# Token stage of a conv and Fourier-mixing block: norm sums of half chunks in single partitions, one row operation on 224 columns

## The chip, the cores and the metric

One NeuronCore of one Trainium2 chip runs the whole kernel. The time is the device time of one launch in microseconds (us). A core has the engines PE (matrix multiplication, with its weight loads shown as PEld), DVE (vector), ACT (scalar activations), POOL (GpSimd) and SP, which here issues every DMA. Each engine works through its own instructions in order; semaphores tie them together.

## The reference

Input `x` is 32 images of 96 channels by 56 x 56 pixels. Layer 0 is a convolution block (1x1, depthwise 3x3 and 1x1 convolutions with batch norms) added to `x`. Layer 1 works on tokens: each image has 3136 tokens of 96 channels.

```
t = _to_tokens(x)                              # (32, 3136, 96)
t = t + attn(_ln_t(t), ...)                    # w1, relu, FFT over tokens, diagonal + relu, inverse FFT, w2
t = t + ffn(_ln_t(t), W1, b1, W2, b2)          # 96 -> 384 -> 96 with fp8-like rounding

def _ln_t(v, eps=1e-5):
    m = jnp.mean(v, axis=-1, keepdims=True)
    s = jnp.var(v, axis=-1, keepdims=True)
    return (v - m) / jnp.sqrt(s + eps)
```

The change is in how the mean and the variance of the two `_ln_t` are made: for each of an image's 3136 tokens a mean and a standard deviation over 96 channels.

## The kernel before

The convolution stages run first, over all images, and leave the input of the last batch norm in HBM. The change is in `tokens_stage`, which then does layer 1 image by image. Channels lie in partitions there and tokens in columns; an image is 7 chunks of CH = 448 columns (`NCH` = 7).

**The pipeline.** An image passes through these steps: load and batch norm (`load_in`, `bn3`, `pool_y`), first norm (`square1`, `mean1`, `var1`, `std1`, `row1`), first product and first half of the FFT (14 groups: `w1`, `rstd1`, `h`, `stage1`, `a`), a round trip of `a` through HBM (`store_a`, `load_b`), spectrum (6 groups: `spectrum`, `scaled`, `real`, `imag`, `relu`, `fold`), product with w2 and first inverse half (8 groups: `w2`, `wz`, `stage3`, `c`), a round trip of `c` through HBM (`store_c`, `load_d`, 4 pieces), `stage4` and `residual` (7 chunks), second norm (`square2`, `mean2`, `var2`, `std2`, `rstd2`, `spread_mean`, `centre`, `spread_rstd`, `norm`) and the two MLP products (`mlp1` 21 times, `mlp2` 7 times, with their copies and biases).

**The order.** The table `PLACES` gives each step a place on a line of 5 x 2000 places. In a turn (there are 36) every engine goes through places 0 to 1999 and at place s does the steps that stand at s, s + 2000, ... s + 8000, the last of these for images that are 1 to 4 behind. So five images are in work at once, and the table fixes the order of instructions on each engine. A place is no time: each engine does its next instruction as soon as its semaphores allow it. Sorted by place, the orders around the first norm are in each turn:

```
PE   ... spectrum 0, mlp2 5, spread_rstd 3, w2 7, mlp1 18, 19, stage3 7, mlp1 20, spectrum 1,
     mean1 0, square1 0, mlp2 6, mean1 1, square1 1, w1 0, spectrum 2, stage4 0, w1 1, stage1 0, ...
ACT  ... mlp2 copy 5, h16 18, 19, relu 0, h16 20, scaled 1, mean1 0, square1 1, mlp2 copy 6, std1 0, relu 1, mean1 1, scaled 2, ...
DVE  ... c 7, bias1 19, fold 0, bias1 20, relu1 6, var1 0, real 1, ...
SP   ... store_c 3, load_t 5, load_in 1, row1 0, load_t 6, load_d 3, store_out, load_b 3, load_in 2, row1 1, ...
```

`h16` is the copy of an `mlp1` result by ACT; `relu1` and `bias1` are the DVE's part of the MLP. `w1 0` waits for the rows that `row1` sends, `stage4 0` for all four `load_d` of its image. `load_d 3` waits on SP for the landing of `store_c 3`, which waits for `c 7` (the DVE's copy of `stage3 7`).

**The sums (lines 1284 to 1316).** PE multiplies a chunk (or its square, made by ACT) with `mean_w[:, 0:32]`, 96 x 32 values of 1/96. Chunk 4r + q goes to output partitions 32q to 32q + 31, all of which get the same row of 448 sums. So round r = 0 takes chunks 0 to 3 and round r = 1 chunks 4 to 6. Means go to PSUM bank `L0`, sums of squares to `L1`. [...]

**The row operations.** For each round ACT squares the means (`m2a`, `m2b`; for the second norm it also copies them to `mrow`), DVE subtracts (line 1661) and clips at zero (line 1663), and ACT takes the root (line 1497 or 1502), all on 128 x 448 or 96 x 448. For the first norm SP then sends one row per chunk to partition 96 of `y` (line 1208), where it meets `w1a`; for the second norm DVE takes the reciprocal (line 1730) and PE spreads mean and reciprocal over 96 partitions by a matmul with one row of ones (`row1`, line 1321), two chunks at a time from two different row groups.

**Waits that matter.** `mean1` round 1 waits for `var1` round 0, since both use `L0`. `square1` round 1 on ACT waits for PE's sums of round 0, since both use the buffer `sq`.

Of the kernel before, what the change touches and what calls it, by code (L numbers as in the profile page):

```python
# [98 lines left out]
def build(nc, x4, cw1, g1, b1, cw2, g2, b2, cw3, g3, b3, aw1, bn1g, bn1b, bn1m, bn1v, ar, ai, arb, aib,
          aw2, bn2g, bn2b, bn2m, bn2v, fw1, fb1, fw2, fb2, t1_d, t4_d, g2_d, g3_d, ident_d, lane_d, out4):  # L100
# [929 lines left out]
PLACES = {'load_in': (0, 143, 286, 429, 571, 714, 863),  # L1030
 'act_bn3': (341, 496, 576, 750, 888, 1052, 1183),
 'pool_y': (362, 517, 597, 771, 909, 1074, 1204),
 'store_t': (1247,),
 'act_square1': (1683, 2129),
 'mean1': (2073, 2154),
 'square1': (2092, 2169),
 'act_mean1': (2117, 2210),
 'dve_var1': (2135, 2289),
 'act_std1': (2171, 2329),
 'row1': (2189, 2347),  # L1040
 'w1': (2289, 2391, 2443, 2495, 2569, 2775, 2860, 2933, 3060, 3116, 3234, 3309, 3398, 3460),
 'dve_rstd1': (2314, 2414, 2466, 2518, 2641, 2820, 2904, 3025, 3084, 3152, 3272, 3331, 3424, 3487),
 'act_h': (2356, 2422, 2474, 2533, 2650, 2830, 2915, 3040, 3098, 3161, 3290, 3367, 3438, 3521),
 'stage1': (2407, 2459, 2585, 2695, 2877, 2949, 3005, 3132, 3266, 3343, 3414, 3476, 3552, 3630),
 'act_a': (2435, 2487, 2634, 2719, 2904, 2973, 3029, 3174, 3313, 3380, 3450, 3533, 3576, 3654),
 'store_a': (2502, 2734, 2988, 3189, 3395, 3548, 3669),
 'load_b': (3765, 3781, 3901, 4264),
 'spectrum': (3897, 4032, 4326, 4731, 5023, 5149),
 'act_scaled': (3948, 4079, 4377, 4797, 5068, 5221),
 'dve_real': (3995, 4159, 4417, 4835, 5110, 5433),  # L1050
 'pool_imag': (3986, 4118, 4415, 4835, 5103, 5250),
 'act_relu': (4030, 4188, 4512, 4866, 5134, 5495),
 'dve_fold': (4058, 4242, 4649, 5041, 5247, 5516),
 'w2': (4511, 4821, 4966, 5189, 5507, 5690, 5795, 5969),
 'dve_wz': (4557, 4867, 5029, 5235, 5571, 5736, 5841, 5990),
 'stage3': (4678, 4894, 5097, 5289, 5594, 5754, 5864, 6007),
 'dve_c': (4722, 4918, 5156, 5334, 5672, 5778, 5928, 6039),
 'store_c': (4934, 5351, 5795, 6048),
 'load_d': (5035, 5481, 6020, 6241),
 'load_t': (5469, 5531, 5706, 5743, 5963, 6068, 6230),  # L1060
 'stage4': (6371, 6424, 6476, 6551, 6602, 6659, 6712),
 'dve_residual': (6397, 6449, 6501, 6576, 6627, 6684, 6737),
 'act_square2': (6595, 6766),
 'mean2': (6621, 6791),
 'square2': (6641, 6807),
 'act_mean2': (6666, 6843),
 'dve_var2': (6698, 6879),
 'act_std2': (6728, 6928),
 'dve_rstd2': (6752, 6958),
 'spread_mean': (6911, 7324, 7611, 7881),  # L1070
 'spread_rstd': (7077, 7379, 7671, 7959),
 'dve_centre': (6930, 6944, 7345, 7359, 7638, 7652, 7908),
 'dve_norm': (7094, 7137, 7396, 7410, 7688, 7708, 7976),
 'mlp1': (7177, 7183, 7228, 7250, 7260, 7283, 7431, 7437, 7493, 7501, 7546, 7569, 7729, 7735, 7771, 7777, 7834, 7840,
          7995, 8001, 8026),
 'act_h16': (7198, 7210, 7244, 7263, 7275, 7303, 7461, 7484, 7510, 7543, 7559, 7586, 7742, 7754, 7783, 7794, 7847,
             7857, 8008, 8020, 8052),
 'dve_bias1': (7216, 7227, 7276, 7284, 7292, 7322, 7478, 7501, 7536, 7583, 7592, 7603, 7760, 7770, 7800, 7811, 7863,
               7873, 8030, 8042, 8086),
 'dve_relu1': (7300, 7373, 7549, 7616, 7820, 7887, 8100),  # L1080
 'mlp2': (7361, 7443, 7576, 7647, 7847, 7941, 8127),
 'act_o': (7389, 7473, 7601, 7671, 7871, 7981, 8159),
 'dve_bias2': (7427, 7490, 7666, 7702, 7922, 8025, 8188),
 'pool_out': (7438, 7502, 7677, 7714, 7934, 8038, 8199),
 'store_out': (8253,)}
# [724 lines left out]
```

## Time and profile before

| | us |
|---|---|
| median of 3 runs (5497.74 to 5525.28) | 5508.2 |
| the profiled execution | 5526.98 |
| its span | 5525.2 |
| PE busy | 5073.0 (92%) |
| DVE busy | 3675.9 (67%) |
| ACT busy | 3496.6 (63%) |
| POOL busy | 2539.9 (46%) |

PE busy time is modelled from pipelined matmuls, so a busy PE need not be one at its peak. The token stage starts at about 2572.85 us (its first DMA) and lasts to the end.

### The profile page before, as it was taken

The page shows a single profiled execution, that of the slowest core. Times are in us where ns is not written, and L with a number is a line of the kernel's source. Part 1 is how long each engine was busy: PE and PEld are TensorE (multiplying, and loading weights), DVE is VectorE, ACT ScalarE, POOL GpSimd, SP SyncE. Part 2 cuts the span into 40 slices and gives each one's busy share as a digit, 9 for nine tenths or more (in the row PEclk, how much of TensorE's full clock was granted, in tenths as well). Part 3 has the DMA queues.
Part 4 walks back from the last instruction along what each step waited for, and adds up shares of the span by engine and source line. Part 5 has one row for each costly group of instructions (what it writes and reads, how often), then busy time and mean ns, then how long its engine had stood idle before and what let it go on. Part 6 is the DMA issues. An engine that isn't in the chain of part 4 may idle for free.

```text
span 5525.2 us, 146982 instructions
## 1 busy us (share of the span) xinstructions
PE 5073.0 (92%) x59604; PEld 3360.4 (61%) x59604; DVE 3675.9 (67%) x6406; ACT 3496.6 (63%) x5895; POOL 2539.9 (46%) x1508
## 2 busy tenths in 40 slices
PE   8999999999999899996798989999999999999986
PEld 8955555555555444443566666666667666666663
DVE  1167776776778667774277777777777676777765
ACT  4456555665665588884466766666667666666652
POOL 0077777777777556663233333333333333333321
PEclk9999999999999999998699999999999999999986
DMA  7667776776776799996456566565565655656441
GB/s 161 154 156 190 180 188 177 191 190 173 187 188 178 233 418 417 419 417 233 139 145 172 153 169 171 159 177 154 167 174 155 169 151 162 171 159 177 144 119 47
DMA packets 500652, 1061.12 MB, mean 192 GB/s; under 512 B 178048, under 2 KB 346976, under 8 KB 466976
## 3 DMA queue, kind: packets, MB, share of 16 engines
q1 hardware_dynamic: 499984, 1051.72, 64.1%
q8 instruction: 479, 7.85, 0.6%
q14 instruction: 189, 1.55, 0.1%
HBM read 552.39 MB, written 478.94 MB: 187 GB/s over the span
## 4 chain that ended last, share of the span: by engine, by line
PE 35%; ACT 5%; DMA 4%; issue 4%; DVE 3%; SPq 1%; POOL 1%; DVEq 0%; POOLq 0%; ACTq 0%
PE bank_w L1412 5%; PE bank_s L1421 5%; PE bank_x L1367 4%; PE bank_o L1392 4%; PE bank_l L1321 4%; DMA bt<-a_scratch 3%; PE bank_c L1375 2%; PE bank_c L1376 2%; PE bank_x L1364 2%; PE bank_o L1403 2%; PE bank_l L1348 2%; ACT h L1487 1%; PE bank_c L1382 1%; DMA y<-va 1%; PE bank_l L1309 1%
## 5 line engine op out<-in xcount | busy, mean ns | idle before, releaser
L762 POOL TENSOR_TENSOR hlo<-h,hhi 128x1682 f16<-128x1682 f32 x288 | 977.4, 3394 | 381.7 <-DVE hhi L815 381.7
L775 DVE BATCH_NORM_STATS2 stats<-z 128x6 f32<-128x392 f32 x1152 | 597.1, 560 | 443.2 <-ACT z L715 433.1
L725 ACT ACTIVATE h<-c1ps,s 128x1568 f32<-128x1568 f32 x288 | 479.1, 1663 | 631.5 <-PE c1ps L641 631.5
L673 PE MATMUL dwps<-hhi,taps 64*64 64x392 f16 x13824 | 692.2, 331 | 11.4 <-issue 11.4
L673 PE MATMUL dwps<-hlo,taps 64*64 64x392 f16 x13824 | 684.2, 328 | 7.4 <-issue 7.4
L1606 POOL TENSOR_TENSOR y<-zin,x_tok 96x448 f32<-96x448 f32 x224 | 254.1, 1135 | 791.1 <-ACT zin L1562 790.8
L1622 POOL TENSOR_TENSOR onat<-tb,o 96x448 f32<-96x448 f32 x224 | 237.7, 1061 | 784.8 <-DVE o L1682 784.8
L920 ACT ACTIVATE z2m<-z2m,s 128x784 f32<-128x784 f32 x512 | 489.3, 1029 | 103.1 <-DMA z2m<-z_scratch 102.8
L1412 PE MATMUL bank_w<-w1a,y 97*112 97x193 f32 x1792 | 410.7, 354 | 137.1 <-DMA y<-va 102.8
L673 PEld LDWEIGHTS dwps<-hhi,taps 64*64 64x64 f16 x13824 | 382.5, 106 | 251.0 <-issue 106.0
L944 POOL TENSOR_TENSOR h_split<-z2m,h_split 128x1568 f16<-128x1568 f32 x128 | 405.1, 3165 | 263.8 <-DVE h_split L983 263.8
L673 PEld LDWEIGHTS dwps<-hlo,taps 64*64 64x64 f16 x13824 | 407.5, 106 | 186.6 <-issue 10.5
L1556 ACT ACTIVATE h<-bank_w,rt 112x192 f32<-112x192 f32 x896 | 326.2, 418 | 206.5 <-PE bank_s L1421 129.9
L1412 PEld LDWEIGHTS bank_w<-w1a,y 97*112 97x112 f32 x1792 | 287.6, 185 | 264.2 <-DMA y<-va 129.9
L1613 POOL TENSOR_TENSOR s_plus<-d_minus,imag_scaled 128x448 f32<-128x448 f32 (+1 forms) x192 | 231.9, 1208 | 470.2 <-ACT imag_scaled L1472 470.2
L1487 ACT ACTIVATE h<-bank_l 128x448 f16<-128x448 f32 x672 | 342.5, 546 | 148.7 <-PE bank_l L1348 145.6
L1421 PE MATMUL bank_s<-h,t1c 112*128 112x192 f32 x1792 | 385.9, 338 | 3.4 <-ACT a L1549 3.4
L1669 DVE TENSOR_SCALAR h<-h,fqb 128x448 f16<-128x448 f16 x672 | 302.1, 468 | 121.4 <-ACT h L1487 108.2
L956 PE MATMUL pps<-z2m,w3T 128*96 128x392 f32 x1024 | 362.5, 497 | 15.1 <-ACT z2m L920 15.1
L193 POOL TENSOR_TENSOR xlo<-xin,x_packed 96x448 f16<-96x448 f32 x224 | 233.9, 1045 | 287.3 <-ACT x_packed L184 286.8
L1375 PE MATMUL bank_c<-w2p,zp 128*112 128x96 f32 x1856 | 347.8, 270 | 12.4 <-DVE cc L1744 12.4
L1549 ACT ACTIVATE a<-bank_s 128x384 f32<-128x384 f32 x448 | 220.3, 492 | 216.0 <-PE bank_s L1421 215.8
(226 smaller groups left out, 10819.1 us busy)
## 6 DMA issues: line engine op xcount, KB each, us to landing
z_scratch<-z SPq DMA_DIRECT2D x1152, 196.0 KB, 3.3
z2m<-z_scratch SPq DMA_DIRECT2D x64, 1960.0 KB, 15.8
z2m<-z_scratch SPq DMA_DIRECT2D x64, 1568.0 KB, 11.5
a_scratch<-a SPq DMA_DIRECT2D x224, 384.0 KB, 2.4
bt<-a_scratch SPq DMA_DIRECT2D x96, 672.0 KB, 7.6
c_scratch<-cc SPq DMA_DIRECT2D x128, 336.0 KB, 3.4
d<-c_scratch SPq DMA_DIRECT2D x128, 336.0 KB, 3.9
xa<-in_x_dram SPq DMA_DIRECT2D x32, 1176.0 KB, 7.5
```

Source lines behind the costliest of these rows:

```text
L673: ins = nc.tensor.matmul(dw[64 * j:64 * j + 64, r, g, 0:QN], taps[half, u, da, dx, :, :].rearrange("p y c -> p (y c)"), part[half, s, a0:a ...
L725: nc.scalar.activation(to, src, ACT.Relu, bias=s1[:, 1, u:u + 1], scale=s1[:, 0, u:u + 1]).then_inc(h_ready, 1)
L762: nc.gpsimd.tensor_tensor(to, h, hi, ALU.subtract).then_inc(lo_ready, 1)
L775: nc.vector.bn_stats(stats[:, i, v, at:at + 6], z2[:, v % 3, g, r, :]).then_inc(s_stat, 1)
L920: nc.scalar.activation(v, v, ACT.Relu, bias=s2[:, 1, t:t + 1], scale=s2[:, 0, t:t + 1]).then_inc(h2_ready, 1)
L944: nc.gpsimd.tensor_tensor(lo, h32, hi, ALU.subtract).then_inc(lo_ready, 1)
L956: nc.tensor.matmul(banks[m], w3T[:, t, :], z2m[:, c // 2, 4 * m + t, cols], start=(t == 0), stop=False)
L1375: nc.tensor.matmul(o, zp[:, k1 // 8 % 2, k1 % 8, :], w2p[:, :], start=True, stop=False)
L1412: ins = nc.tensor.matmul(WB[0:TP, 0, e * (H + 1):(e + 1) * (H + 1)], y[:, par, 2 * g + e, :, :].rearrange("p a b -> p (a b)"), w1a[:, :], ...
L1421: ins = nc.tensor.matmul(SB[:, 0, e * H:e * H + H], t1c[:, 2 * g + e, :], h[:, g % 2, e * H:e * H + H], start=True, stop=True)
L1487: nc.scalar.activation(h16[:, c % 2, q, :], LL[k % 2][:, 0, 0:CH], ACT.Copy).then_inc(h16_done, 1)
L1556: nc.scalar.activation(h[:, g % 2, e * H:e * H + H], WB[0:TP, 0, e * (H + 1):e * (H + 1) + H], ACT.Relu, scale=rt[:, g % 2, e, :]).then_in ...
```

## The change

One matmul now has a half chunk of HC = 224 columns, and a table of weights puts its sums into a single partition: column 33j of `mean_w` holds 1/96 and the rest zero, so `mean_w[:, 32j:32j + 32]` has its only ones column at j. Half k of chunk c lands in partition 32 (c % 4) + j, j = 2 (c // 4) + k, and four matmuls (two for q = 3) accumulate into one block of 32 partitions. All 14 half chunks of an image lie then in one bank in 224 columns, and every row operation runs once, on 128 x 224. The spreading matmul takes four partitions of the row tile and picks one by `sel`.

```
+    sel = (p[:, None, None] % 32 == np.arange(4)[None, :, None]) * np.ones((1, 1, C))
-                link(nc.vector.memset(mean_w[:, :], 1.0 / C))
+                link(nc.vector.memset(mean_w[:, :], 0.0))
+                link(nc.vector.memset(mean_w[:, 0:128:33], 1.0 / C))
-    m2a = sb("m2a", [128, CH])            # va, m2b the same
+    m2a = sb("m2a", [128, HC])
-    mrow = sb("mrow", [128, 2, CH])       # rrow the same
+    mrow = sb("mrow", [128, HC])
+    def sums_of(r):
+        for j in (2 * r, 2 * r + 1):
+            for c in chunks_of(r):
+                q, k = c % 4, j % 2
+                yield q, j, c, k, (j == 0), (j == (3 if q < 3 else 1))
...
+    def load_row(sp, f, par):
+        sp.wait_ge(std1_done, f + 1)
+        settled(sp)
+        v = y[C:C + 1, par, :, :, :].rearrange("p (c k j) a b -> p c k (j a b)", k=2, j=2)
+        for r in range(2):
+            n = len(chunks_of(r))
+            for k in range(2):
+                i = 2 * r + k
+                sp.dma_start(v[:, 4 * r:4 * r + n, k, :], va[i:i + 32 * n - 31:32, :]).then_inc(ld_row, 16)
...
+        for r in range(2):                    # mean1_tensor, no wait between the rounds
+            for q, j, c, k, first, last in sums_of(r):
+                rows = y[0:C, par, 4 * c + 2 * k:4 * c + 2 * k + 2, :, :].rearrange("p j a b -> p (j a b)")
+                ins = nc.tensor.matmul(L0[32 * q:32 * q + 32, 0, 0:HC], mean_w[:, 32 * j:32 * j + 32], rows,
+                                       start=first, stop=last)
...
-            ins = nc.tensor.matmul(LL[c % 2][0:C, 0, 0:CH], row1[32 * q:32 * q + 1, :], rows[32 * q:32 * q + 1, r, :],
-                                   start=True, stop=True)
+        for k in range(2):
+            for c in pair_of(p):
+                q, j = c % 4, 2 * (c // 4) + k
+                ins = nc.tensor.matmul(LL[c % 2][0:C, 0, k * HC:k * HC + HC], sel[32 * q:32 * q + 4, j, :],
+                                       rows[32 * q:32 * q + 4, :], start=True, stop=True)
...
-        if g in (0, 8):
-            pe.wait_ge(ld_row, f * 16 * NCH + (64 if g == 0 else 112))
+        if g == 0:
+            pe.wait_ge(ld_row, (f + 1) * 64)
-        nc.scalar.activation(m2a[0:w, :], L0[0:w, 0, 0:CH], ACT.Square).then_inc(m1_done, 1)
+        nc.scalar.activation(m2a[:, :], L0[:, 0, 0:HC], ACT.Square).then_inc(m1_done, 1)
-        nc.vector.tensor_tensor(v, L1[0:w, 0, 0:CH], m2[0:w, :], ALU.subtract).then_inc(var_done, 1)
+        nc.vector.tensor_tensor(v, L1[:, 0, 0:HC], m2[:, :], ALU.subtract).then_inc(var_done, 1)
-        nc.vector.reciprocal(rrow[0:w, r, :], rrow[0:w, r, :]).then_inc(rs_done, 1)
+        nc.vector.reciprocal(rrow[:, :], rrow[:, :]).then_inc(rs_done, 1)
```

The squares of the norms are still made in two rounds, into the same buffer. The squaring of the means on ACT now waits for the means alone, and `var1`, `var2` on DVE for that and for both rounds of sums. `sel` is loaded by one more DMA at the start of the stage; the memset of `row1` is gone.

The whole table `PLACES` is replaced. The PE's order stays nearly the same as a cycle; what differs around the first norm is:

```
PE   ... spectrum 0, spread_rstd 3, stage3 6, mlp1 18, 19, w2 7, mlp2 5, mlp1 20, spectrum 1, stage3 7,
     mean1, square1 0, square1 1, mlp2 6, spectrum 2, stage4 0, w1 0, w2 0, w1 1, stage1 0, ...
ACT  ... scaled 0, mlp2 copy 4, h16 18, 19, 20, mlp2 copy 5, relu 0, scaled 1, square1 1, mean1, std1, mlp2 copy 6, relu 1, scaled 2, ...
DVE  ... bias1 18, w2 copy 7, bias1 19, fold 0, c 7, bias1 20, relu1 6, real 1, var1, bias2 5, fold 1, ...
SP   ... store_c 3, load_in 0, load_t 2, load_d 3, row1, load_t 3, 4, 5, load_in 1, load_t 6, load_in 2, 3, store_a 0, load_in 4,
     store_out, store_a 1, load_b 3, ...
```

The second norm's order on PE is `mean2 0, square2 0, stage4 5, stage1 3, w1 5, stage4 6, spectrum 3, mean2 1, square2 1, w2 1, stage1 4, spread_mean 0, w1 6, stage3 1, spectrum 4, stage1 5, w1 7, spread_rstd 0`; DVE does `centre 0, rstd1 6, rstd2, centre 1` within it. On SP `load_b 0` follows `store_a 6` with `load_d 1` between, where it had `load_t 2` and `load_t 3`.

## Rows read from the trace of the kernel before

**Rows 1.** Windows of one turn's length, a steady one and the last: busy us, instructions.
```profile
core 0: us, PE busy (x) PEld busy (x) DVE busy (x) ACT busy (x) POOL busy (x), PEclk, DMA share, GB/s
...
3814.50:3899.80 85.30, 77.74 (x547) 56.27 (x546) 62.52 (x120) 58.81 (x116) 29.11 (x26) 0.98 0.58 166
...
5435.20:5520.50 85.30, 51.59 (x166) 20.33 (x166) 38.80 (x71) 22.46 (x40) 9.40 (x10) 0.55 0.12 35
```

**Rows 2.** Who waited for whom, PE in ten turns: total us, times, longest.
```profile
PE bank_w L1412 <- DMA y<-va: 33.1, 10, 4.0
...
PE bank_o L1403 <- issue: 8.4, 8, 1.1
```

**Rows 3.** PE in order of time, one turn: start us, length us, [idle before].
```profile
3867.55 2.04 PE L1367 MATMUL bank_x<-g2c,bt 112*128 112x112 f32 x16 [0.83 <-DMA bt<-a_scratch]
...
3870.09 0.99 PE L1321 MATMUL bank_l<-rrow,row 1*96 1x448 f32 x2
3871.01 0.44 PE L1375 MATMUL bank_c<-w2p,zp 128*112 128x96 f32 x2
...
3873.37 1.75 PE L1364 MATMUL bank_x<-g2c,bt 112*64 112x112 f32 x32
3875.05 0.96 PE L1291 MATMUL bank_l<-y,mean_w 96*32 96x448 f32 x8
3875.83 0.94 PE L1296 MATMUL bank_l<-sq,mean_w 96*32 96x448 f32 x8
3877.83 0.74 PE L1403 MATMUL bank_o<-hq,fq 128*96 128x448 fp8e5 x3 [1.06 <-issue]
...
3883.38 0.91 PE L1412 MATMUL bank_w<-w1a,y 97*112 97x193 f32 x4 [3.18 <-DMA y<-va]
3884.13 3.14 PE L1367 MATMUL bank_x<-g2c,bt 112*128 112x112 f32 x16
3887.06 1.41 PE L1392 MATMUL bank_o<-t4c,d 128*96 128x112 f32 x8
3888.31 0.82 PE L1412 MATMUL bank_w<-w1a,y 97*112 97x193 f32 x4
```

**Rows 4.** The other engines in order of time, the same stretch.
```profile
3874.37 0.32 SPq L1223 DMA_DIRECT2D c_scratch<-cc  x1
...
3876.41 0.63 ACT L1472 ACTIVATE imag_scaled<-bank_x,diag 128x448 f32<-128x448 f32 x1
...
3876.92 0.55 ACT L1530 ACTIVATE m2a<-bank_l 128x448 f32<-128x448 f32 x1
...
3877.34 1.32 ACT L1512 ACTIVATE sq<-y 96x1344 f32<-96x1344 f32 x1
3877.64 0.62 DVE L1661 TENSOR_TENSOR va<-bank_l,m2a 128x448 f32<-128x448 f32 x1
...
3879.05 0.66 ACT L1497 ACTIVATE va<-va,epsc 128x448 f32<-128x448 f32 x1
...
3879.79 2.40 SPq L1208 DMA_DIRECT2D y<-va  x4
...
3882.93 0.35 SPq L1230 DMA_DIRECT2D d<-c_scratch  x1
```

**Rows 5.** Line 1223 (store of c), eight issues in two turns: time to landing.
```profile
DMA to landing us min/median/max: 3.1/4.6/9.5
```

**Rows 6.** Line 1230 (load of d), eight issues in two turns: time to landing.
```profile
DMA to landing us min/median/max: 3.5/4.1/6.9
```

**Rows 7.** Groups of instructions by form from 3000 us on: busy us, mean ns.
```profile
L1730 DVE RECIPROCAL rrow<-rrow 128x448 f32<-128x448 f32 x29 | 85.2, 2938 | 0.0
...
L1663 DVE TENSOR_SCALAR rrow<-rrow 96x448 f32<-96x448 f32 x29 | 36.8, 1267 | 1.0
...
L1309 PEld LDWEIGHTS bank_l<-tb,mean_w 96*32 96x32 f32 x406 | 9.0, 108 | 11.2 <-issue 7.8
```

**Rows 8.** Line 1218 (load_b 3), the issue at 3883.86: time to landing.
```profile
DMA to landing us min/median/max: 10.3/10.3/10.3
```

More of the change, by code:

```diff
@@ L47 @@
 NP4 = NJ // 4
+HC = CH // 2
 def wait_count(eng, sem, value):
@@ L1029 @@
 LAGS = 5
[L1030 to L1085, printed above, removed]
@@ L1100, in tokens_stage @@
     g3c = sb("g3c", [TP, TP])
-    row1 = sb("row1", [128, C])
+    sel = sb("sel", [128, 4, C])
     zin = sb("zin", [C, 3, CH])
@@ L1261, in sync_turn @@
                 load_b(sp, tau - lag, k)
-            for r, lag in here(s, "row1", live):
-                load_row(sp, tau - lag, (par + lag) % 2, r)
+            for _, lag in here(s, "row1", live):
+                load_row(sp, tau - lag, (par + lag) % 2)
             for c, lag in here(s, "load_in", live):
@@ L1293, in square1_tensor, with square_sums @@
+        ins.then_inc(mean1_full, 1)
+    def square_sums(pe, r):
+        for q, j, c, k, first, last in sums_of(r):
+            ins = nc.tensor.matmul(L1[32 * q:32 * q + 32, 0, 0:HC], mean_w[:, 32 * j:32 * j + 32],
+                                   sq[:, q, k * HC:k * HC + HC], start=first, stop=last)
+        return ins
     def square1_tensor(pe, f, r):
         pe.wait_ge(sq1_done, f * 2 + r + 1)
-        for q, c in enumerate(chunks_of(r)):
-            ins = nc.tensor.matmul(L1[32 * q:32 * q + 32, 0, 0:CH], mean_w[:, 0:32], sq[:, q, :], start=True, stop=True)
@@ L1312, in square2_tensor @@
+        pe.wait_ge(t2_done, b * NCH + min(4 * r + 4, NCH))
+        for q, j, c, k, first, last in sums_of(r):
+            at = c * CH + k * HC
+            ins = nc.tensor.matmul(L0[32 * q:32 * q + 32, 0, 0:HC], mean_w[:, 32 * j:32 * j + 32], tb[:, at:at + HC],
+                                   start=first, stop=last)
+        if r == 1:
+            ins.then_inc(mean2_full, 1)
     def square2_tensor(pe, b, r):
         pe.wait_ge(sq2_done, b * 2 + r + 1)
-        for q, c in enumerate(chunks_of(r)):
-            ins = nc.tensor.matmul(L1[32 * q:32 * q + 32, 0, 0:CH], mean_w[:, 0:32], sq[:, q, :], start=True, stop=True)
@@ L1436, in tensor_turn @@
                 stage4_tensor(pe, tau - lag, c)
-            for r, lag in here(s, "mean1", live):
-                mean1_tensor(pe, tau - lag, (par + lag) % 2, r)
+            for _, lag in here(s, "mean1", live):
+                mean1_tensor(pe, tau - lag, (par + lag) % 2)
             for r, lag in here(s, "square1", live):
```

217 lines of the change are left out of this document (126 added, 91 removed).

## The prediction

> **What bounds the kernel now.** I read the windows first. In the token stage a turn takes 85.3 us, and in a steady one PE is busy for 77.74 us, DVE for 62.52, ACT for 58.81, POOL for 29.11 [rows 1]. No engine but PE is near its end, so work taken from DVE and ACT shortens nothing by itself: it counts only where PE waits at the end of a chain that runs through it. PE still has some 7.6 us without work in a turn. The waits say where: 3.3 us (33.1 in ten turns) before the first w1, for the transfer of the standard deviations into `y`, and 0.8 before the last mlp2 [rows 2]. The PE's order of time shows that place. Between the end of spectrum 1 and w1 1 (I call the first E = 3875.05; w1 1 starts at 3888.31) there are 13.26 us [rows 3]. Behind E stand four groups of sums of 0.77 each, mlp2 6 with 0.66, w1 0 with 0.75, spectrum 2 and stage4 0. The last two are slow: after the 3.18 us of waiting spectrum 2 takes 2.93 to the next start, where the 16 records of spectrum 0 took 1.88 to theirs (3867.55 to 3869.43, its length of 2.04 less the overlap of records); stage4 0, half as many records of the same columns, takes 1.25, where by that row it would take some 0.8 to 0.9 at full clock. So for about 3 us PE ran at the lower of its two levels (1.2 instead of 2.4 GHz), which cost some 1.5 us; the window's mean of 0.98 of the granted clock [rows 1] agrees in size, 2% of 85.3 us being 1.7. So the place costs 4.5 us of idling and 1.5 us of clock; the other some 3 us of idling are spread in pieces under 1 us and do not touch the norms.
>
> The last view is that of the other engines [rows 4]. It gives the chain behind the stall: sums end at 3876.77, `m2a` starts 0.15 later, DVE subtracts for 0.62, clips, ACT takes the root for 0.66 and ends at 3879.71, SP issues four row transfers from 3879.79 in 2.40 us, and w1 0 starts at 3883.38: 3.6 us from the first issue.
>
> **The change, part by part.** The sum is for one turn.
>
> *Row operations.* DVE does in a turn four subtractions (0.62), four clippings (0.4 to 1.27) and two reciprocals (2.94) [rows 4, 7], 11 us with 2.8 for the clippings. Halved in number and in width, each operation left costs between a half and the whole of its time; I take 0.40, 0.27 and 1.55, nearer the half since the reciprocal's time goes with its columns: 2.9 us. So DVE gets back 8 us of 62.5. ACT has ten operations of 0.55 to 0.66 [rows 4]; five remain, of some 0.37 to 0.47 by the same bounds: 5.9 us become 2.1. Both engines are off the bound, so I cost this at nothing but what it does to the chain below, and take 0.1 us off for small waits behind busy queues (bounds 0 and 0.8).
>
> *Sums on PE.* 28 matmuls of 448 columns become 56 of 224, 56 records become 112, each with a weight load. Eight records of 448 columns, four column groups, take 0.77 and six take about the same, so the groups run beside each other and columns set the time [rows 3]. Half the columns in twice the records give the same, if records can follow each other fast enough: 8 records in 0.385 us is 48 ns each. The shortest spacing in the trace is that of spectrum 1, 32 records from 3873.37 to 3875.05, 53 ns each [rows 3]. At 53 ns the four rounds of 16 records cost 0.85 instead of 0.77, and those of 12 records 0.64, less than the 0.75 of their columns: +0.3 us at most from spacing, 0 at least. The other bound is a weight load that nothing hides: 56 more of 0.108 [rows 7], +6.0 us. I take +0.1, from the spacing row.
>
> What bears on this is that the weight loads were hidden before: eight records with eight loads fit into 0.77 us, which the two passes over 448 columns of each group fill alone [rows 3]. The Trainium skill, TensorE: Matmul & The Clock Gate, section "Part 3: Packing small matmuls — row/col tiling", says that a weight load runs beside matmuls in flight only when its row group differs, and the sums differ only in column groups. By that rule the added loads would stand on the path; by the row they don't, as far as 448 columns tell. It makes the last rival below.
>
> *Spreading.* 14 matmuls of 448 columns with one row become 28 of 224 with four. One chunk alone takes 0.92 (3870.09 to 3871.01) [rows 3]; the weights of 96 columns are now loaded twice as often, again behind streams of half the length. Bounds 0 and 0.8 us over eight spreadings; I take 0.1.
>
> *The first norm's place.* Order on PE after: spectrum 1, stage3 7, means, squares 0, squares 1, mlp2 6, spectrum 2, stage4 0, w1 0, w2 0, w1 1. All times from E. stage3 7 takes 0.25, 14 sums 1.5, squares 0 0.77: E + 2.5, sums ended at 2.7. ACT can square round 1 only then, because of the buffer `sq`; nothing stands between the two groups on PE, so the 1.32 of the squaring, with 0.15 before it and some 0.2 behind, is idle time on PE: squares 1 start at 4.3 and end at 5.2. Before, mlp2 6 and the means of round 1 lay there. Then DVE subtracts (0.2 + 0.40) to 5.8, clips to 6.2, ACT takes the root to 6.7, SP issues at 6.8, and with the 3.6 of before the rows are there at 10.4. SP has four transfers as w1 0 needed before; the three others go. Two waits grow: on ACT the root now holds back mlp2's copy 6, relu 1 and scaled 2 (0.54, 0.94 and 2.1, done by 10.4), which h 0 needs only after w1 0; on DVE `var1` holds back bias2 5, on which the output 5 and load_t 5 wait. Behind the waiting `row1` on SP stand load_t 3 to 5 and load_in 1, which move to about 10.7; their users (residual 0, bn3 1) come at 14 and 17, so 3 us remain with landings of a few us.
> The second chain ends at the same point. relu 0 on ACT comes after mlp2's copy 5 and ends near E + 0.6, fold 0 on DVE to 1.8, c 7 to 2.1, store_c 3 at 2.2, landing 4.6 later at 6.8 [rows 5]; load_d 3 lands 4.1 later at 10.9 [rows 6]. Before, the store went out at E - 0.7 and the load at E + 7.9, behind `row1` [rows 4]. Now stage4 0 stands before w1 0 and waits for it. PE has in the meantime 0.66 and 1.8 of work behind squares 1 and is idle from 7.7 on. I let stage4 0 start at 10.6, between the ends of the two chains (bounds 8.8 and 18.6, by the shortest and the longest landings). Then come stage4 0 (0.8), w1 0 (0.75) and w2 0, with 1.5 us of lower clock as before, since the stall is again 3 us long: 13.65 without w2 0. Less stage3 7, which stood ahead of E before: 13.4 against 13.26, +0.15.
>
> *Ahead of E.* From the end of spectrum 0 (3869.43) to E are 5.6 us, with two idle pieces of 0.4 before and between the mlp1's. In the new order stage3 6 and the ends of mlp1 18 and 19 lie between the spreading and what needs it, w2 7 and mlp2 5 before mlp1 20: I take 0.5 of the 0.7 back, bounds 0 and 0.7.
>
> *Second norm.* mean, root and reciprocal run once, 1.5 us later on PE than round 0 did, but spread_mean 0 has w2 1 and stage1 4 in front of it (2.3 us) against 0.9 of chain from the sums, and spread_rstd 0 has 5 us of PE work against 3.4 (centre 0, reciprocal 1.55, centre 1). Covered; if the cover went it would cost the difference, nothing here. load_b 3 now goes out behind store_a 1, near E + 28.5, and spectrum 4 comes near 36.8: 8.3 us of room.
>
> *Sum.* Per turn -0.1 + 0.1 + 0.1 + 0.15 - 0.5 = -0.25, with a doubt of 0.7 us either way from the landings, the clock and the pieces. 31 turns lie between the first image's sums and the last's: -8 us. In the first three turns there is no stage4 and hardly a spectrum to lie under the longer chain of the first norm: +2. The drain, the last turn with a clock of 0.55 [rows 1], has one short reciprocal instead of two on the path, but centre 1 now waits behind it: 0. Total -6 us: 5527.0 of the profiled execution becomes 5521. That execution was the slowest of those shown, 18.8 above the median; I carry the difference over: 5508.2 - 6 = 5502.
>
> **The rivals.**
> *A, the stall breaks up (5446).* If the store of c lands in 3.1 and the load in 3.5, the shortest seen [rows 5, 6], stage4 0 starts at 8.8 and only the rows are late, behind 0.8 us more of work; two waits of under 2 us may leave the clock up, as the 1.06 before mlp2 6 did [rows 3]. Against the kernel before that is 0.8 us of idling and 1.2 of clock, 2.0 a turn: 31 x 2.0 = 62. For it: the new order puts 2.5 us of work under the chain. Against: the medians.
> *B, the load of d comes late (5567).* Slower. load_d 3 stands ahead of `row1` on SP and before w1 0 on PE, so what delays it delays all. With landings of 5.5 and 5.3 instead of 4.6 and 4.1 (the longest are 9.5 and 6.9 [rows 5, 6]) it lands at 13.0 instead of 10.9 and costs 1.9 us a turn, 59 in all. It decides from a landing past E + 10.6; each us more is a us per turn. For it: SP must now wait for that landing with other loads behind it. Against: the medians do not come near those lengths.
> *C, load_b 3 comes late (5548).* It took 10.3 us [rows 8], against 8.3 of room: 1.5 a turn, 46 in all. Against: then it was issued right behind the output store, which now lies 10 us ahead.
> *D, the added weight loads are not hidden (5688).* +6.0 a turn by the load's duration [rows 7], 31 x 6.0 = 186 on the forecast. Against: eight loads were hidden behind eight records before [rows 3].
>
> **How the numbers follow.** Forecast (own range 5482 to 5528, from 0.7 us a turn) 0.42, A 0.29, B 0.19, C 0.07, D 0.03. Within 0.5% (27.5 us, about what a measurement can tell from no change) is 5481 to 5536: nearly all of the forecast and a part of B and C, which go over into it. Faster: A and 0.04 of the forecast, 0.33. Slower: D, and most of B and C, 0.24. Same: the rest, 0.43. The range 5440 to 5560 leaves out D, the upper part of B and the lower end of A.
>
> **What would show it.** Steps: 16 + 12 records of sums in 1.5 to 1.7 us; a wait of 1.5 us on PE before squares 1, put to ACT's squaring; stage4 0 and w1 0 both behind a wait that ends within 0.5 us of E + 10.6, and slow; row operations in one set per norm, DVE near 54 and ACT near 55 us a turn; PE busy unchanged. Wrong: a turn under 84.3 or over 86.3 us; a wait for `load_d` over 4 us; spectrum 4 waiting for `bt`.

## The result and the profile after

The changed kernel takes 5317.4 us (5303.8 to 5321.8, four runs), the kernel before 5503.0 in the runs beside it: ratio 0.965, 95% interval 0.962 to 0.969. That is 186 us less; the forecast was 6 us less, 5502, and its range ended at 5440. The profiled execution went from 5525.2 to 5316.8 us of span, 208 us less, since the one of before was the slowest of its kernel; sums over a whole trace, below, are to be held against the 208.

From the page of the changed kernel; the 40 slices are 133 us each.

```profile
span 5316.8 us, 151659 instructions
...
PE 4976.9 (94%) x62292; PEld 3460.3 (65%) x62292; DVE 3393.8 (64%) x6246; ACT 3409.9 (64%) x5735; POOL 2564.3 (48%) x1508
...
PEclk9989999999999999999789999999999999999996
```

Two turns of the token stage, to hold against the first window of [rows 1]:

```profile
core 0: us, PE busy (x) PEld busy (x) DVE busy (x) ACT busy (x) POOL busy (x), PEclk, DMA share, GB/s
3860.30:3941.10 80.80, 76.90 (x631) 61.46 (x630) 53.70 (x116) 55.97 (x110) 29.63 (x26) 0.98 0.62 176
3941.10:4022.00 80.90, 75.84 (x633) 60.10 (x632) 53.86 (x117) 55.97 (x110) 29.63 (x26) 1.00 0.62 176
```

A turn is 80.8 us where it was 85.3; the prediction had called a turn under 84.3 a sign that it was wrong. PE's work is nearly what it was (75.8 to 76.9 against 77.7, less where the granted clock is 1.00); its idle time went from 7.6 to 3.9 and 5.1. DVE has 53.7 (forecast 54), ACT 56.0 (forecast 55).

Between the starts of the first and the last image's sums lie 2665.7 us before (2600.1 to 5265.8) and 2471.9 after (2602.9 to 5074.8). The first two of these 31 intervals were 80.3 and 78.3 us and are 63.8 and 68.7: 26 us. The 29 others were 86.5 on average and are 80.7: 168 us. The typical turns give 4.5 of these 5.8 us; the rest is that before had seven turns of 87.8 to 90.9 us among them, where the longest after is 85.4. What follows the last image's sums, some three turns long, went from 259.4 to 242.0, another 17 us.

The block in which the forecast placed the change: PE in order of time (start us, length us, idle before), from E, the end of spectrum 1, here 3867.55, to hold against [rows 3].

```profile
3867.55 0.43 PE L1401 MATMUL bank_c<-wz,g3c 112*112 112x96 f32 x2
3867.91 1.52 PE L1304 MATMUL bank_l<-y,mean_w 96*32 96x224 f32 x25
...
3869.30 1.08 PE L1310 MATMUL bank_l<-sq,mean_w 96*32 96x224 f32 x15
3871.89 0.96 PE L1310 MATMUL bank_l<-sq,mean_w 96*32 96x224 f32 x12 [1.51 <-ACT sq L1529]
3872.78 0.77 PE L1422 MATMUL bank_o<-hq,fq 128*96 128x448 fp8e5 x3
3873.38 1.94 PE L1386 MATMUL bank_x<-g2c,bt 112*128 112x112 f32 x16
3876.24 1.01 PE L1411 MATMUL bank_o<-t4c,d 128*96 128x112 f32 x8 [0.93 <-DMA d<-c_scratch]
3877.94 1.25 PE L1431 MATMUL bank_w<-w1a,y 97*112 97x193 f32 x4 [0.69 <-DMA y<-va]
...
3881.87 0.83 PE L1431 MATMUL bank_w<-w1a,y 97*112 97x193 f32 x4
```

In place of the stall of 3.18 us there are three waits of 1.51, 0.93 and 0.69. Spectrum 2 is 1.94 long where it was 3.14, the length that its 16 records have at the higher of the clock's two levels (2.4 GHz; 2.04 in [rows 3]), and stage4 0 is 1.01 long and not 1.41. stage4 0 comes at E + 8.7 instead of E + 10.6. w1 0 comes at E + 10.4, where the forecast had the rows land; w1 0 itself it had at 11.4, behind its later stage4 0. The other engines of the same block, against [rows 4]:

```profile
3869.17 0.30 SPq L1235 DMA_DIRECT2D c_scratch<-cc  x1
3870.51 1.32 ACT L1529 ACTIVATE sq<-y 96x1344 f32<-96x1344 f32 x1 [0.99 <-PE bank_l L1310]
3872.61 0.30 SPq L1242 DMA_DIRECT2D d<-c_scratch  x1
3872.96 0.39 DVE L1676 TENSOR_TENSOR va<-bank_l,m2a 128x224 f32<-128x224 f32 x1 [1.35 <-ACT m2a L1546]
3873.39 0.28 DVE L1678 TENSOR_SCALAR va<-va 128x224 f32<-128x224 f32 x1
3873.70 0.48 ACT L1515 ACTIVATE va<-va,epsc 128x224 f32<-128x224 f32 x1 [1.62 <-DVE va L1678]
3874.27 2.59 SPq L1220 DMA_DIRECT2D y<-va  x4
```

The store goes out at E + 1.6; 3.4 us later the load of d is issued, and 3.6 after that stage4 0 starts. The row transfers go at E + 6.7.

PE's waits in 1400 us (3500 to 4900: 17 turns of after, 16 of before), total, times, longest; first the kernel before, then the changed one:

```profile
PE bank_w L1412 <- DMA y<-va: 52.9, 16, 4.0
PE bank_l L1348 <- ACT h L1487: 14.0, 30, 0.6
PE bank_o L1403 <- issue: 13.6, 13, 1.1
PE bank_w L1412 <- ACT h L1556: 8.8, 17, 0.5
PE bank_x L1367 <- DMA bt<-a_scratch: 7.2, 11, 1.3
PE bank_c L1375 <- DVE cc L1744: 6.2, 16, 0.4
PE bank_l L1348 <- DVE yq L1702: 5.3, 14, 0.4
```

```profile
PE bank_l L1310 <- ACT sq L1529: 25.7, 17, 1.5
PE bank_o L1411 <- DMA d<-c_scratch: 15.0, 13, 1.5
PE bank_l L1367 <- ACT h L1506: 9.1, 17, 0.5
PE bank_w L1431 <- DMA y<-va: 7.1, 16, 0.8
PE bank_o L1411 <- DVE tb L1727: 6.1, 11, 1.1
```

Two things are to be seen. The wait for y, 3.3 us a turn, is 0.4. And small waits have gone too: for ACT's h of w1 (line 1556), for cc, nearly all for yq, most of those for bt; together 24 us of the 1400, or 1.5 a turn. The forecast had taken off 0.1 a turn for small waits behind busy queues and 0.5 for the pieces ahead of E.

### The profile page after: what moved, and what is told of

Read it like the earlier page. It is cut to its first block, busy times and chain, and to the rows that moved or that the text cites. A ratio compares the mean times of both kernels' runs of the same rounds, so it can differ in the third digit from the quotient of the medians.

```text
span 5316.8 us, 151659 instructions
## 1 busy us (share of the span) xinstructions
PE 4976.9 (94%) x62292; PEld 3460.3 (65%) x62292; DVE 3393.8 (64%) x6246; ACT 3409.9 (64%) x5735; POOL 2564.3 (48%) x1508
## 3 DMA queue, kind: packets, MB, share of 16 engines
q14 instruction: 184, 1.51, 0.1%
## 4 chain that ended last, share of the span: by engine, by line
PE 41%; DMA 3%; issue 2%; SPq 2%; ACT 1%; DVE 1%; POOL 0%; POOLq 0%; DVEq 0%; ACTq 0%
PE bank_w L1431 6%; PE bank_s L1440 5%; PE bank_l L1339 4%; PE bank_c L1394 4%; PE bank_o L1411 3%; PE bank_c L1395 3%; PE bank_c L1401 3%; PE bank_x L1386 3%; PE bank_l L1367 3%; PE bank_o L1422 2%; PE bank_x L1383 2%; PE bank_l L1310 1%; DMA tb<-t_scratch 1%; SPq L1220 1%; PE bank_l L1326 1%
## 5 line engine op out<-in xcount | busy, mean ns | idle before, releaser
L677 PE MATMUL dwps<-hhi,taps 64*64 64x392 f16 x13824 | 693.8, 331 | 11.4 <-issue 11.2
L1637 POOL TENSOR_TENSOR onat<-tb,o 96x448 f32<-96x448 f32 x224 | 260.1, 1161 | 513.0 <-DVE o L1697 513.0
L1431 PE MATMUL bank_w<-w1a,y 97*112 97x193 f32 x1792 | 386.5, 338 | 26.6 <-DMA y<-va 21.6
L1440 PE MATMUL bank_s<-h,t1c 112*128 112x192 f32 x1792 | 375.0, 332 | 2.3 <-ACT a L1564 2.3
L1395 PE MATMUL bank_c<-w2q,zq 128*112 128x96 f32 x1856 | 347.2, 270 | 0.0
L1431 PEld LDWEIGHTS bank_w<-w1a,y 97*112 97x112 f32 x1792 | 289.7, 179 | 62.5 <-DMA y<-va 28.3
```

The lines of the kernel that those rows point to most:

```text
L677: ins = nc.tensor.matmul(dw[64 * j:64 * j + 64, r, g, 0:QN], taps[half, u, da, dx, :, :].rearrange("p y c -> p (y c)"), part[half, s, a0:a ...
L1395: ins = nc.tensor.matmul(o, zq[:, k1 // 2 % 8, :], w2q[:, e * C:e * C + C], start=False, stop=True)
L1431: ins = nc.tensor.matmul(WB[0:TP, 0, e * (H + 1):(e + 1) * (H + 1)], y[:, par, 2 * g + e, :, :].rearrange("p a b -> p (a b)"), w1a[:, :], ...
L1440: ins = nc.tensor.matmul(SB[:, 0, e * H:e * H + H], t1c[:, 2 * g + e, :], h[:, g % 2, e * H:e * H + H], start=True, stop=True)
```

## The experiments

Each ran beside the kernel before on one chip, in batches on different chips; its ratio is to the kernel before of its own batch. Waits are PE's in 3500 to 4900 unless another engine is named. Places are the numbers by which each engine's order is made.

**One half of the change at a time.** *The order alone*: the two-round tiles of before in the places of after, second rounds right behind the first.

```diff
-  (the places of before)
+  (the places of after, and for the second rounds:)
+  'mean1': (2891, 3020), 'act_mean1': (2848, 2879), 'dve_var1': (2860, 2888), 'act_std1': (2878, 2890),
+  'row1': (2421, 2422), 'act_mean2': (7300, 7335), 'dve_var2': (7318, 7343), 'act_std2': (7333, 7498),
+  'dve_rstd2': (7344, 7511),
```

> The kernel before with its sums, tiles and row operations in two rounds, but in the new table of places (the second rounds stand right behind the first, at the places of the single ones). Theory 1, the order carries the gain (work of PE put under the chain of the first norm, fewer small waits): at least two thirds of the 185 us remain, 5380 us or less, a turn of some 82 us. Theory 2, the merged row operations carry it (8.8 us less DVE and 2.8 us less ACT work in a turn, a shorter chain): 5440 us or more, since two chains of 448 columns then stand behind each other on DVE and ACT.

*The tiles alone*: the changed kernel in the places of before.

```diff
-  (the places of after)
+  (the places of before, and:)
+  'mean1': (2073,), 'act_mean1': (2130,), 'dve_var1': (2160,), 'act_std1': (2171,), 'row1': (2189,),
+  'act_mean2': (6843,), 'dve_var2': (6879,), 'act_std2': (6928,), 'dve_rstd2': (6958,),
```

> The changed sums and row operations in the order of before (the merged operations at the places of the second round's sums and the first round's root and transfer). Theory 1: little is gained or it is slower, 5470 to 5560 us, since the row chain now begins only behind both rounds of squares and w1 0 follows at once: the wait for the transfer grows from 3.2 to about 5 us. Theory 2: 5350 to 5420 us.

Measured: the order alone 5671.0, ratio 1.030 (1.027 to 1.032); the tiles alone 5577.8, 1.012 (1.008 to 1.016). Each half makes the kernel slower (the second by more than its expectation allowed, 5470 to 5560), together they make it 3.5% faster. The waits, first of the order alone, then of the tiles alone:

```profile
PE bank_o L1389 <- ACT o L1489: 53.3, 15, 3.8
PE bank_w L1409 <- ACT h L1553: 39.4, 16, 2.5
PE bank_o L1389 <- DVE tb L1709: 24.1, 16, 1.6
PE bank_l L1288 <- DVE va L1658: 19.8, 15, 1.3
```

```profile
PE bank_w L1428 <- DMA y<-va: 76.6, 15, 5.4
...
PE bank_c L1391 <- DVE cc L1755: 6.3, 16, 0.4
PE bank_l L1364 <- DVE yq L1714: 4.9, 13, 0.4
```

The new order closes two rounds of row operations right in front of stage4 and w1, and PE then waits for ACT and DVE. The new tiles in the old order make the rows ready later (one set, after both groups of sums), with nothing of PE's in front of w1 0: 5.1 us a turn instead of 3.3. The first intervals tell whose the 26 us of the fill are: 61.6 and 69.7 with the order alone, 85.0 and 77.4 with the tiles alone. They are the order's. The small waits divide too. With the order alone none for cc, yq or bt is left, but 39.4 for h of w1; with the tiles alone those for cc, yq and bt (6.3, 4.9 and 6.7) are what they were, and the one for h of w1 (8.8 before) is gone. So the first three went by the order, and by shorter row operations only the last.

**Which places matter.** In the kernel before, w1 0 behind stage4 0:

```diff
-  'w1': (2289, 2391, 2443, 2495, 2569, 2775, 2860, 2933, 3060, 3116, 3234, 3309, 3398, 3460),
+  'w1': (2372, 2391, 2443, 2495, 2569, 2775, 2860, 2933, 3060, 3116, 3234, 3309, 3398, 3460),
```

> The kernel before with one step moved: w1 0 stands on PE behind spectrum 2 and stage4 0 instead of ahead of them. Theory 1: spectrum 2 and the wait for the load of d fill the wait for the transfer, so the 3.2 us of idling and the lower clock behind it shrink by 2 to 3 us a turn: 5410 to 5450 us. Theory 2: the order of these three is not what counts, 5480 us or more.

Then also load_d 3 ahead of row1 on SP:

```diff
-  'load_d': (5035, 5481, 6020, 6241),
+  'load_d': (5035, 5481, 6020, 6188),
```

> The kernel before with two steps moved: w1 0 behind spectrum 2 and stage4 0 on PE (slower by 3% alone), and load_d 3 ahead of the first row transfers on SP. Theory 3: now spectrum 2 and stage4 0 lie under the row chain, the 3.2 us wait and the low clock behind it go, 2 to 4 us a turn: 5390 to 5450 us. If the old two-round row operations stand in the way by themselves: 5490 us or more.

Then also w2 0 between w1 0 and w1 1:

```diff
-  'w2': (4511, 4821, 4966, 5189, 5507, 5690, 5795, 5969),
+  'w2': (4380, 4821, 4966, 5189, 5507, 5690, 5795, 5969),
```

> The kernel before (two rounds, tiles of 448 columns) with three places moved: w1 0 behind stage4 0, load_d 3 ahead of row1 on SP (both as in the run before_two_moves, 5517.7 us, where w1 1 waited 43.4 us for ACT's h 0, 33 waits in 3500 to 4900), and now w2 0 between w1 0 and w1 1. Theory that the order alone, once PE has something to do while ACT turns out h 0, brings a part of the gain without new tiles: the wait of 2.9 us a turn in that run goes, 5400 to 5450. Rival, that the two-round norm needs DVE and ACT too long in any order: the wait only moves (to w2 0 for h 0), 5490 or more.

And in the changed kernel, the load of d put back behind the rows:

```diff
-  'load_d': (5633, 5989, 6212, 6421),
+  'load_d': (5633, 5989, 6212, 6422),
```

> The changed kernel with one step moved on SP: load_d 3 behind the row transfers instead of ahead of them. Theory 3, the order of PE and the order of SP only pay together: load_d 3 is then issued 4 us later (E + 9.3 for E + 5.1), stage4 0 starts at E + 13, 4 us later, in front of w1 0: 31 x 3 to 4 us, 5410 to 5450 us. If the load of d does not matter: within 0.5% of 5317 us.

Measured in this order: 5673.8, ratio 1.030 (1.026 to 1.033); 5517.7, 1.001 (0.999 to 1.003); 5466.8, 0.992 (0.989 to 0.995); and 5468.3, 0.993 (0.991 to 0.996). One line of waits of each:

```profile
PE bank_o L1389 <- DMA d<-c_scratch: 70.7, 15, 5.8
```

```profile
PE bank_w L1409 <- ACT h L1553: 43.4, 33, 2.5
```

```profile
PE bank_w L1409 <- ACT h L1553: 26.5, 48, 1.0
```

```profile
PE bank_o L1408 <- DMA d<-c_scratch: 92.2, 17, 5.6
```

The gain that was expected of the three kernels from before (at most 5450 each) came in none; the last was expected at 5410 to 5450 and lost more. So the place of one load on SP is worth 151 us in the changed kernel and 156 in the first pair. With it the wait for the rows is broken up in the old tiles as well, but the time is given back in a wait for h. The third move lowers that only in part, and so the order alone, as far as I could mend it for the old tiles, is worth 36 of the 186 us.

**DVE's time.** The changed kernel with useless reciprocals of 128x448 (2.94 us each) on DVE: three a turn (behind var1, behind var2, behind centre 1); then only the last two; then two at other places where DVE was idle, behind var1 and behind the last residual.

```diff
+    def burn_b(dve, b, i):
+        wait_count(dve, s_burn_b, b * 2 + i)
+        nc.vector.reciprocal(burn2[:, :], ones_c[:, :]).then_inc(s_burn_b, 1)
...
```

> The changed kernel with the freed DVE time taken up again: three reciprocals of 448 columns a turn on tiles that nobody reads (8.8 us), one behind each clipping and one behind centre 1. If the load of DVE is what made the small waits in the rest of the turn, they come back: 2 to 4 us a turn, 5380 to 5440 us. If only order and chain length count, it stays within 1% of 5317 us.

> The changed kernel with two useless reciprocals of 128x448 a turn on DVE (5.9 us, both in the second norm; none in the chain from var1 to rstd1 0, where the run dve_load had its third one). Theory that freed time of DVE as such is worth several us a turn: PE waits for ACT's h and for cc as in dve_load, 5370 to 5420. Rival, that the 127 us of that run came from the one reciprocal in the first norm's chain (2.94 us on the path): within 0.5% of the changed kernel, 5300 to 5345.

> The changed kernel with the same 5.9 us of useless work a turn on DVE as in the run dve_load_no_chain (two reciprocals of 128x448), but at two other places: one behind var1, one behind the last residual, where DVE is idle for 1.6 and 2.8 us before its next instruction. In dve_load_no_chain both lay between the small reciprocals rt of the w1 groups, and ACT waited 164 us for rt instead of 71.8 (3500 to 4900). Theory that what counts is how long DVE's queue holds up the rt, not how much DVE has to do: 5310 to 5350. Rival, that DVE's total counts: 5420 to 5450.

Measured: 5444.2, 5441.3 and 5323.8 (ratios 0.988, 0.988 and 0.966; the last one's interval, 0.963 to 0.969, is that of the changed kernel). The third reciprocal, in the first norm's chain, added nothing that can be measured, and the same 5.9 us a turn cost 124 us at one place and nothing that can be measured at the other. Why is to be seen in ACT's waits for the little reciprocals rt, which scale h behind each w1; the kernel before, the changed kernel, then the load between the rt (5441.3), then the load in the gaps:

```profile
ACT h L1556 <- DVE rt L1688: 35.7, 58, 1.0
```

```profile
ACT h L1571 <- DVE rt L1703: 71.8, 87, 2.5
```

```profile
ACT h L1575 <- DVE rt L1707: 164.0, 117, 3.6
...
PE bank_w L1435 <- ACT h L1575: 28.9, 32, 1.2
```

```profile
ACT h L1575 <- DVE rt L1707: 78.5, 85, 3.8
...
3500.00:4900.00 1400.00, 1321.36 (x10781) 1047.87 (x10779) 1042.15 (x2011) 962.84 (x1894) 521.39 (x446) 0.98 0.61 174
```

A 2.94 us instruction in DVE's queue holds an rt of 0.17 up, that holds h up on ACT, and PE waits for h. In the last kernel DVE is busy for 1042 us of the 1400, more than in the kernel before (1017), and it is as fast as the changed one. It is not how much DVE does. Nor is it the second norm's own chain, in which both reciprocals of the slow kernel stand: PE's waits there name neither yq nor the rows rrow, but 28.9 us for h and 11.6 for cc. Of its 3.9 us more a turn 2.8 are idle time of PE, the rest is longer work at a granted clock of 0.98 instead of 0.99.

This is the price of long instructions in the new order. In the kernel before ACT waited less for rt (35.7) than in the changed one, and PE 8.8 us for h, 0.5 a turn.

The test from the other side: the best two-round kernel above (5466.8) with DVE's row operations on half the columns (half the variances stay at one; everything else unchanged).

```diff
+        v = v[:, 0:CH // 2]
-        nc.vector.tensor_tensor(v, L1[0:w, 0, 0:CH], m2[0:w, :], ALU.subtract).then_inc(var_done, 1)
+        nc.vector.tensor_tensor(v, L1[0:w, 0, 0:CH // 2], m2[0:w, 0:CH // 2], ALU.subtract).then_inc(var_done, 1)
...
-        nc.vector.reciprocal(rrow[0:w, r, :], rrow[0:w, r, :]).then_inc(rs_done, 1)
+        nc.vector.reciprocal(rrow[0:w, r, 0:CH // 2], rrow[0:w, r, 0:CH // 2]).then_inc(rs_done, 1)
```

> The run before_w2_early (two rounds, the best order found for them, 5466.8 us) with DVE's subtractions, clippings and reciprocals of both norms on 224 of the 448 columns, so that half of the variances are left at one and the output is another one; ACT, PE and the transfers unchanged. It takes some 4.2 us a turn from DVE, 2.8 of them in the reciprocals that stand between the rt. Theory that long row operations in DVE's queue are what the old tiles cost: PE's wait for h falls, 5380 to 5430. Rival, that the old tiles cost by their two rounds of sums, squares and roots on PE and ACT: 5450 or more.

Measured: 5412.7, ratio 0.984 (0.982 to 0.986), 54 us under the kernel that it stems from, inside the expectation. PE's wait for h:

```profile
PE bank_w L1410 <- ACT h L1554: 14.1, 35, 0.6
```

It was 26.5. So halving DVE's row operations takes 54 us off the old tiles in a mended order, or 45 by the ratios of the two batches, and the load puts 124 onto the new. The edit also shortens both norms' chains (PE's wait for va at the means fell from 7.2 to 2.7), so that the 54 are not the queue's alone. The 124 are too high a bound for what the shorter operations are worth: with the load, DVE has 2 x 2.94 and its own 1.53 at those places, the kernel before 2 x 2.94.

**What is left at the block.** Two buffers for the squares, so that squares 1 need not wait for ACT (both norms; the waits on `sq` are taken out to match):

```diff
-    sq = sb("sq", [C, 4, CH])
+    sq = sb("sq", [C, NCH, CH])
...
-  'act_square1': (2469, 2849),
+  'act_square1': (2469, 2470),
```

> The changed kernel with a buffer `sq` for all seven chunks, so that ACT squares both rounds ahead of time and the 1.5 us of waiting between squares 0 and 1 on PE goes. If PE's idle time in the block counts as it stands: the row chain begins 1.5 us earlier, but the load of d (E + 8.7) is then what stage4 0 waits for and w1 0 starts at about E + 9.5 instead of 10.4: 0.9 us a turn, 5285 to 5295 us. If the wait only moves on to the load of d and the clock falls there: 5310 to 5325 us.

Measured: 5322.0, ratio 0.966 (0.963 to 0.969): nothing.

```profile
PE bank_o L1408 <- DMA d<-c_scratch: 47.9, 17, 3.4
```

The wait for sq (25.7) is gone and the wait for d rose from 15.0 by 32.9: what PE waits in all is the same (63 us of 1400, 66 before the edit). Waits of about a microsecond became one of 2.8 on average, and the granted clock of the window fell from 0.99 to 0.97, PE's busy time rose from 1329.6 to 1333.3. Then the transfers of c and d, on top of the two buffers: stage3 7 and c 7 earlier, and load_t 2 to 4 issued ahead of load_d 3, while SP waits for the store of c to land (the second expectation below says "behind row1"; by their places and in the trace they go ahead of both); and the same without moving stage3 7:

```diff
-  'load_t': (5805, 6175, 6420, 6478, 6608, 6611, 6838),
+  'load_t': (5805, 6175, 6418, 6419, 6420, 6611, 6838),
   (first kernel)  'stage3' 7: 6871 -> 6830, 'dve_c' 7: 6826 -> 6811
   (second kernel) 'dve_c' 7: 6826 -> 6824
```

> The kernel with the two square buffers and the chain of the d load begun earlier: stage3 7 ahead of spectrum 1 on PE, c 7 ahead of fold 0 on DVE (so store_c 3 leaves about 2.5 us earlier), load_t 3 and 4 ahead of load_d 3 on SP. The load of d then lands before E + 7 and the rows at E + 9.2: 1.2 us a turn less than the changed kernel, 5275 to 5285 us. If it is instead the rate of w1, rstd1 and h on ACT that binds behind w1 0, no more than the kernel with the buffers alone.

> The changed kernel with two buffers of sq, c 7 ahead of fold 0 on DVE and load_t 2 to 4 behind row1, stage3 7 left where it is. In the run with two buffers alone stage4 0 waited 47.9 us for d (17 waits in 3500 to 4900, 2.8 each). The store of c goes out some 0.8 us earlier. Theory that the transfers of c and d now set the end of this place: the wait for d falls by 0.6 to 0.8 a turn, 5285 to 5305. Rival, that PE's clock takes it back (short waits, lower clock) or that the row chain ends as late: 5315 to 5325.

Measured: 5304.9, ratio 0.963 (0.961 to 0.966), and 5296.6, 0.962 (0.959 to 0.964). The first gave back what it gained: stage3 7 then waited for wz (15.1 us, 16 times), the wait for d was 36.9. The second had 38.4 for d and no wait for wz, but 8.3 for d_minus. The first missed its expectation. Its interval and the second's both overlap that of the changed kernel, so that neither gain is clear of noise.

Last, on top of the second of these, more of PE's work under these waits: relu 1 earlier on ACT, w2 0 and stage4 1 to 6 earlier on PE, and residual 0 waiting for five of the loads of t and not for six:

```diff
-  'act_relu': (4776, 4912, 5162, 5590, 5917, 6384),
+  'act_relu': (4776, 4877, 5162, 5590, 5917, 6384),
-  'w2': (5082, 5409, 5667, 5877, 6071, 6298, 6527, 6794),
+  'w2': (5070, 5409, 5667, 5877, 6071, 6298, 6527, 6794),
...
-  'stage4': (7072, 7121, 7143, 7219, 7258, 7313, 7338),
+  'stage4': (7072, 7074, 7120, 7140, 7219, 7258, 7313),
...
-            dve.wait_ge(ld_t, (b + 1) * 16 * (NCH - 1))
+            dve.wait_ge(ld_t, (b + 1) * 16 * (NCH - 2))
```

> As the run c_before_fold, and more of PE's work under the two waits: w2 0 ahead of stage4 0's group, stage4 1 to 6 moved ahead, relu 1 ahead of std1 on ACT, residual 0 waiting for its own five loads only. Theory that what is left at this place is want of work for PE: waits for d and for y fall by 1.5 to 2 us a turn more, 5255 to 5285. Rival, that relu 1 ahead of std1 holds back the rows, or that the stage4 moved ahead finds its d later: 5310 or more.

Measured: 5244.6 (5242.0 to 5246.3), ratio 0.952 (0.951 to 0.954), better than the expectation and the best of all kernels run. Its window and its longest wait:

```profile
3500.00:4900.00 1400.00, 1352.83 (x11223) 1071.23 (x11222) 981.23 (x2044) 996.92 (x1963) 545.11 (x466) 1.00 0.63 180
...
PE bank_o L1408 <- DMA d<-c_scratch: 10.0, 15, 1.2
```

PE is busy for 96.6% of the time at a granted clock of 1.00; a turn is 78.1 us in the middle of the stage.

## Why the prediction was wrong

*The step that failed* is how the parts were priced: each by itself, against the waits of one turn of the kernel before. Two terms carry most of the error. The 29 turns from the third image's sums on are 5.8 us shorter on average; the forecast had 0.25.

*The block at the first norm*, forecast +0.15, measured -2.7. From the start of the sums to w1 1 it was 14.04 us on average over these turns and is 12.93, or 11.37 without w2 0, which stood elsewhere before (1.56 at full clock). The forecast took the old block from one turn, 13.26; the block is 13.1 to 13.5 in 11 of 30 turns and 14.1 to 15.1 in 19, and in 18 of these 19 spectrum 2 is 3.6 us long behind the stall, where it is 3.14 in the turn shown. Two steps in it were wrong. One is the chain of c and d: in the turn shown the store went out at E + 1.6 and not 2.2, and both transfers took 7.1 us and not 8.7 (medians of 39 issues of all pieces in ten turns: 4.0 and 4.2), so that stage4 0 started at E + 8.7; over the turns it is E + 9.0, near rival A's 8.8. The other is the 1.5 us of lower clock, which the forecast kept since "the stall is again 3 us long": PE's idle time in the block is still 3.13 us in the turn shown, but in three pieces, and in 20 of 30 turns w1 0 and w2 0 behind it run at full clock (0.91 for w1 0 in the turn from 3948.36 on). In the turn shown, one of the ten others, they don't (1.25, and 2.88 for w2 0). The row chain was right (10.39 against 10.4), squares 1 too (4.34 against 4.3). So A's mechanism, which I had held for the less likely, came true, as part of a gain three times its size.

*The rest of the turn*, forecast -0.4 in all (0.5 and 0.1 off, twice 0.1 on), measured -3.1. PE's idle time outside the block fell from 2.96 to 1.17 us on average, and its work there became shorter by the other 1.3, as fits the higher granted clock (0.96 over the 1400 us before, 0.99 after). The forecast had looked for the order's gain only between spectrum 0 and E; the waits for cc, yq and bt lie in other parts of the turn too, and the order took them away. It had read the windows as "No engine but PE is near its end, so work taken from DVE and ACT shortens nothing by itself" and allowed 0.1 us a turn (bounds 0 and 0.8) for small waits behind busy queues. A busy share (DVE 62.5 of 85.3) says nothing of how long a queue holds up what stands in it: the load between the rt costs 4.0 us a turn and in the gaps none, and DVE's shorter operations are worth some 50 us, or 1.7 a turn, to the old tiles in a mended order. In the old order as it was they would have fitted the bounds (PE waited 0.5 a turn for h); the forecast had priced them by the old order, and the change brings another. I had counted the chains of the two norms, and not who else stood in the queue behind the long reciprocals: the rt, h of ACT, and at their end w1 and stage1 on PE. The irregular turns, which the typical turn leaves out, were 1.3 us on average: the trace of before has them as waits of 1.1 to 1.2 us for bt and a spectrum at lower clock behind (3.76 us for 16 records).

*Fill*: forecast +2, measured -26, the order's as the half alone shows. Before, w1 took some 1.6 us at lower clock 11 times of 14 in the first turn, with waits for h between them; after, 0.91 or less ten times of 14. I had looked for the longer norm chain there and not for what the other places of the diff would do to a turn without stage4. *Drain*, forecast 0: the turns that follow the last sums shorten too, 17 us that the 31 turns leave out. With 168 in the 29 turns and 26 in the two before, less 3 for a later start of the first sums, that is the 208 us between the two traces.

*Right* were the small terms of PE. The 28 means and 16 squares run from 3867.91 to 3870.38, 44 records in 2.47 us with the last one's own length of 0.35; the starts lie 49 ns apart on average (2.12 us for the 43 spacings), inside the forecast's 2.27. That refutes rival D. The Trainium skill, TensorE: Matmul & The Clock Gate, section "Part 3: Packing small matmuls — row/col tiling", says that a weight load overlaps with matmuls in flight only when its row group differs. Here the trace disagrees: 56 added loads of some 0.11 us, which differ in column groups alone, stay hidden, or a turn would be 6 us longer. Rival B did not come, but what it rests on is real: the load of d put one place later costs 151 us. Rival C did not come (bt: 2.6 us in 1400). The sum adds up as it stands. The prices of B and C do not quite follow from their times: 13.0 against 10.9 is 2.1 and not 1.9 a turn, 10.3 against 8.3 is 2.0 and not 1.5; neither came, and nothing hangs on it.

*What the 186 us are*, as far as it was taken apart in steps from before: three places of the order -36, short row operations on DVE -54, and -95 for what is left between that kernel and the changed one. By the ratios, each to the runs of before in its own batch, the three are 42, 45 and 104, so that each is known to some 10 us. Of the last step 20 are in the first two intervals (77.8 and 74.8 against 63.8 and 68.7). The rest, about 2.8 us a turn (83.5 on average against 80.7), is one round instead of two on ACT and in the chains together with the remaining places; this was not separated, and no run put ACT's freed time back. Neither half stands alone, so that any split depends on the order of the steps: by their ratios 163 and 64 slower each, 186 faster together.

## What to carry to other kernels

A queue that runs in order is a resource beside its busy share: before costing an edit on an engine "off the bound" at nothing, list the short instructions that stand behind its longest ones and who waits for them, across the chains, not within one. An order and a tiling that were made for each other are judged only together. And a wait taken from the bound engine is no gain until the next wait behind it has been made shorter too, or work has been put under it.

## What the hardware showed that I had not expected

The same 5.9 us of DVE work a turn cost 124 us or nothing by its place. Reciprocals go with their columns: 2938 ns for 448, 1534 for 224 [rows 7]; subtraction (620 against 392) and the first norm's root (660 against 482) do so only in part [rows 4]. With the same sum of waits in longer pieces the granted clock was 0.97 instead of 0.99 (two buffers for the squares), and with hardly any over a microsecond it was 1.00 (the best kernel). And half-length records in four column groups started 49 ns apart, weight loads and all.
